# Expert layers' routing: every third token tile's row marks on GpSimd, and roundings to tiles in units of rows

## The reference

```python
gate_logits = jnp.einsum('bsd,de->bse', x, gate_kernel)
top_k_weights, top_k_indices = jax.lax.top_k(gate_logits, TOP_K)
top_k_weights = jax.nn.softmax(top_k_weights.astype(jnp.float32), axis=-1)
h0 = jnp.einsum('bsd,edm->bsem', x, wi_0)
h1 = jnp.einsum('bsd,edm->bsem', x, wi_1)
h = jax.nn.silu(h0) * h1 * combine_w[..., None]
out = jnp.einsum('bsem,emd->bsd', h, wo)
```

## Time and profile before

| | us |
|---|---|
| median of three runs | 1566.65 |
| the three runs | 1563.93, 1566.65, 1568.6 |
| the profiled execution's own time | 1566.98 |
| its span on the core | 1565.2 |

### The profile page before, as it was taken

The page is one execution under the profiler, slowest core; times in us unless marked ns, Lnnn a source line. Parts: engine busy times, 40 slices in busy tenths (PEclk is TensorE's granted clock), DMA queues, the critical chain, the costliest instruction groups (busy, mean ns, idle before and its releaser), DMA issues. The chain is left out here.

```text
span 1565.2 us, 29271 instructions
## 1 busy us (share of the span) xinstructions
PE 1348.1 (86%) x7991; PEld 842.9 (54%) x7992; DVE 1026.3 (66%) x2409; ACT 803.1 (51%) x2370; POOL 627.0 (40%) x660
## 2 busy tenths in 40 slices
PE   5889996798689787999979999988996999969993
PEld 3555553466444353666555666654873666645662
DVE  5898986577569847223656888875335888863224
ACT  4677674687410055331107888843442888823330
POOL 3112420999477232771012111113536664215661
PEclk9999998999799789998998999998996999988997
DMA  6130001400100060794200000331552111412225
GB/s 191 46 113 23 19 12 58 162 0 1 37 17 0 5 211 18 239 286 155 88 17 28 24 23 23 107 122 35 157 134 75 56 43 34 175 55 66 83 83 168
DMA packets 96447, 124.80 MB, mean 80 GB/s; under 512 B 11117, under 2 KB 76464, under 8 KB 96112
## 3 DMA queue, kind: packets, MB, share of 16 engines
q1 hardware_dynamic: 85760, 95.80, 19.2%
q0 software_dynamic: 10608, 28.07, 6.3%
HBM read 91.31 MB, written 33.43 MB: 80 GB/s over the span
## 5 line engine op out<-in xcount | busy, mean ns | idle before, releaser
L717 ACT ACTIVATE l0a_prob<-l0a_ps_s,l0a_neg_max 128x128 f32<-128x128 f32 x512 | 137.9, 398 | 70.6 <-DVE l0a_neg_max L559 63.1
L717 ACT ACTIVATE l2a_prob<-l2a_ps_s,l2a_neg_max 128x128 f32<-128x128 f32 x512 | 138.7, 402 | 26.2 <-DVE l2a_neg_max L559 21.5
L219 POOL TENSOR_TENSOR ln_rstd<-ln_var_eps,minus_half 128x4 f32<-128x4 f32 (+1 forms) x14 | 23.1, 1660 | 246.7 <-POOLq L183 216.3
L1160 ACT ACTIVATE l3a_prob<-l3a_ps_s,l3a_neg_max 128x256 f32<-128x256 f32 x256 | 104.5, 482 | 34.0 <-DVE l3a_neg_max L1074 32.5
L559 DVE TENSOR_REDUCE l2a_neg_max<-l2a_ps_s 128x4 f32<-128x512 f32 x128 | 85.7, 684 | 19.8 <-PE l2a_ps_s L815 18.9
L502 POOL TENSOR_TENSOR l2a_k_head<-l2a_kT,head_of_row 128x512 f32<-128x512 f32 x32 | 33.1, 1054 | 157.7 <-DMA l2a_kT<-k_rows 157.7
L568 DVE COPY l0a_probT<-l0a_ps_t 128x512 f32<-128x512 f32 x128 | 84.7, 683 | 14.5 <-PE l0a_ps_t L827 14.4
L1074 DVE TENSOR_REDUCE l3a_neg_max<-l3a_ps_s 128x2 f32<-128x512 f32 x128 | 84.1, 681 | 12.6 <-PE l3a_ps_s L1211 11.7
L559 DVE TENSOR_REDUCE l0a_neg_max<-l0a_ps_s 128x4 f32<-128x512 f32 x128 | 85.5, 683 | 8.9 <-PE l0a_ps_s L815 8.3
L502 POOL TENSOR_TENSOR l0a_k_head<-l0a_kT,head_of_row 128x512 f32<-128x512 f32 x32 | 32.9, 1048 | 138.0 <-DMA l0a_kT<-k_rows 138.0
L1833 PE MATMUL l1a_ps_y<-l1a_kv,l1a_tap 128*128 128x512 f32 x192 | 84.0, 600 | 3.7 <-POOL l1a_kv L1805 3.7
(11 more groups left out here) (490 smaller groups left out, 3493.7 us busy)
## 6 DMA issues: line engine op xcount, KB each, us to landing
expert_results<-zeros SPq DMA_DIRECT2D x1, 8320.0 KB, 26.3
l1f_got<-expert_results SPq DMA_DIRECT2D x16, 512.0 KB, 3.9
expert_results<-l2f_y_sb SPq DMA_DIRECT2D x47, 128.0 KB, 1.7
l1f_w_gu<-in_l1f_w_gu SPq DMA_DIRECT2D x16, 352.0 KB, 6.7
l2f_w_gu_all<-in_l2f_w_gu SPq DMA_DIRECT2D x1, 4096.0 KB, 14.0
l3f_w_gu_all<-in_l3f_w_gu SPq DMA_DIRECT2D x1, 4096.0 KB, 13.9
l3f_got<-expert_results SPq DMA_DIRECT2D x16, 256.0 KB, 5.2
l1f_w_d<-in_l1f_w_d SPq DMA_DIRECT2D x16, 176.0 KB
```

The lines of the kernel that those rows point to most:

```text
L717: last = act.activation(prob[4 * c + j][:, r * P:r * P + P], ps_s[j][:, r * P:r * P + P], ACT.Exp, bias=neg_max[:, j, r:r + 1])
L1160: last = act.activation(prob[4 * c + j][:, m * D:m * D + D], ps_s[j][:, m * D:m * D + D], ACT.Exp, bias=neg_max[:, j, m:m + 1])
```

## The change

Two edits, in all three expert layers.

Row marks: token tiles 2, 5, 8, 11 and 14 are marked by GpSimd, the other eleven by VectorE. GpSimd waits for slot_done, which the slot_row instruction now raises, does its five tiles in order with K instructions each after its first shared multiplications and before it waits for row_out, and keeps the same rule of the ring. TensorE waits for row_marked or for row_marked_by_pool by the tile. slot_row is now the negative of the row, and lane counts down to match.

Roundings: MAGIC_ROWS = 128 * MAGIC rounds a number of rows straight to a multiple of 128. tiles, ends and base are then in rows: the counts take two instructions where they took three, the base needs no multiplication, and slot_tile takes one where it took two and keeps MAGIC_ROWS in it. It is compared with tile_at = 128 * tile_no + MAGIC_ROWS, which one added instruction makes ahead of the wait for place_put. In L2F and L3F one instruction and a drain are added behind the row marks, which divide ends by 128 for the owners. The hunk left out names the two new semaphores.

```diff
--- before.py
+++ after.py
@@ -1286,6 +1286,7 @@
 
 
 MAGIC = 1.5 * 2.0 ** 23
+MAGIC_ROWS = MAGIC * P
 
 
 def hadamard_ffn(core, name):
@@ -1937,7 +1938,7 @@
             from_slot = sb("from_slot", [P, B, K], U32)
         slot_tile, slot_row = sb("slot_tile", [P, B, K]), sb("slot_row", [P, B, K])
         lane, row_of = sb("lane", [P, P], BF16), sb("row_of", [P, 1])
-        tile_no = sb("tile_no", [P, NT])
+        tile_no, tile_at = sb("tile_no", [P, NT]), sb("tile_at", [P, NT])
         in_row = [sb(f"in_row{u}", [P, K, P], BF16) for u in range(RING)]
         marks = sb("marks", [P, B * K, NT], BF16)
         got = [got_all[:, r * K * D:(r + 1) * K * D].rearrange("p (k d) -> p k d", k=K) for r in range(NG)]
@@ -1996,12 +1997,12 @@
...
@@ -2156,7 +2157,7 @@
 
             pool.affine_select(out=before[:, :], in_=before[:, :], compare_op=ALU.is_gt, fill=0.0, base=0,
                                pattern=[[1, P]], channel_multiplier=-1).then_inc(const_done, 1)
-            for out, pattern, rowwise in ((tile_no, [[1, NT]], 0), (lane, [[1, P]], 0), (row_of, [[0, 1]], 1)):
+            for out, pattern, rowwise in ((tile_no, [[1, NT]], 0), (lane, [[-1, P]], 0), (row_of, [[0, 1]], 1)):
                 pool.iota(out[:, :], pattern, base=0, channel_multiplier=rowwise,
                           allow_small_or_imprecise_dtypes=True).then_inc(const_done, 1)
             if not capacity:
@@ -2170,6 +2171,14 @@
 
             for n in range(bounds[2]):
                 shared_mul(n)
+            pool.wait_ge(slot_done, 1)
+            for t in range(2, B, 3):
+                if t >= RING:
+                    pool.wait_ge(tokens_put, t - (RING - 1))
+                for k in range(K):
+                    last = pool.tensor_scalar(in_row[t % RING][:, k, :], lane[:, :], slot_row[:, t, k:k + 1], 1.0,
+                                              ALU.is_equal, ALU.mult)
+                last.then_inc(row_marked_by_pool, 1)
             pool.wait_ge(row_out, B // 4 * 16)
             def put_results(j):
                 if j == 0:
@@ -2283,23 +2292,20 @@
             dve.tensor_tensor(weight[:, :, :], top[:, :, 0:K], best.broadcast_to([P, B, K]), ALU.subtract)\
                .then_inc(max_done, 1)
 
+            dve.tensor_scalar(tile_at[:, :], tile_no[:, :], float(P), MAGIC_ROWS, ALU.mult, ALU.add)
             dve.wait_ge(place_put, 1)
             if capacity:
                 where = ps_p[:, 0:B * E].rearrange("p (t e) -> p t e", t=B)
             else:
 
                 dve.wait_ge(counted, 1)
-                dve.tensor_scalar(tiles[:, :], ps_l[:, 0:E], 127.0, 1.0 / P, ALU.add, ALU.mult)
-                dve.drain()
-                dve.tensor_scalar(tiles[:, :], tiles[:, :], 1.0 / 256 - 0.5, MAGIC, ALU.add, ALU.add)
-                dve.drain()
-                dve.tensor_scalar(tiles[:, :], tiles[:, :], MAGIC, None, ALU.subtract)
+                dve.tensor_scalar(tiles[:, :], ps_l[:, 0:E], (P - 1) / 2, MAGIC_ROWS, ALU.add, ALU.add)
+                dve.drain()
+                dve.tensor_scalar(tiles[:, :], tiles[:, :], MAGIC_ROWS, None, ALU.subtract)
                 dve.drain()
                 dve.tensor_tensor_scan(ends[:, :], ones_e[:, :], tiles[:, :], 0.0, ALU.mult, ALU.add)
                 dve.drain()
                 dve.tensor_tensor(base[:, :], ends[:, :], tiles[:, :], ALU.subtract)
-                dve.drain()
-                dve.tensor_scalar(base[:, :], base[:, :], float(P), None, ALU.mult)
                 dve.drain()
                 dve.tensor_tensor(place[:, :, :], ps_p[:, 0:B * E].rearrange("p (t e) -> p t e", t=B),
                                   base[:, :].unsqueeze(1).broadcast_to([P, B, E]), ALU.add)
@@ -2322,16 +2328,14 @@
                 dve.tensor_tensor(spot[:, :, :], spot[:, :, :], flag[:, :, :], ALU.add)
                 dve.drain()
 
-            dve.tensor_scalar(slot_tile[:, :, :], spot[:, :, :], 0.5 - P / 2, 1.0 / P, ALU.add, ALU.mult)
-            dve.drain()
-            dve.tensor_scalar(slot_tile[:, :, :], slot_tile[:, :, :], MAGIC, MAGIC, ALU.add, ALU.subtract)
+            dve.tensor_scalar(slot_tile[:, :, :], spot[:, :, :], (1 - P) / 2, MAGIC_ROWS, ALU.add, ALU.add)
             dve.drain()
             with nc.allow_low_precision(reason="whole numbers under 256"):
-                dve.tensor_tensor(marks[:, :, :], tile_no[:, :].unsqueeze(1).broadcast_to([P, B * K, NT]),
+                dve.tensor_tensor(marks[:, :, :], tile_at[:, :].unsqueeze(1).broadcast_to([P, B * K, NT]),
                                   slot_tile[:, :, :].rearrange("p t k -> p (t k)").unsqueeze(2)
                                   .broadcast_to([P, B * K, NT]), ALU.is_equal).then_inc(tile_marked, 1)
-                dve.scalar_tensor_tensor(out=slot_row[:, :, :], in0=slot_tile[:, :, :], scalar=-float(P),
-                                         in1=spot[:, :, :], op0=ALU.mult, op1=ALU.add)
+                dve.scalar_tensor_tensor(out=slot_row[:, :, :], in0=slot_tile[:, :, :], scalar=MAGIC_ROWS,
+                                         in1=spot[:, :, :], op0=ALU.subtract, op1=ALU.subtract).then_inc(slot_done, 1)
                 dve.drain()
                 dve.tensor_scalar(in_tile[:, 0, :, :], marks[:, :, :], row_of[:, :], None, ALU.mult)\
                    .then_inc(row_scaled, 1)
@@ -2345,10 +2349,13 @@
                 last.then_inc(row_marked, 1)
 
             for t in range(B):
-                mark_rows(t)
+                if t % 3 < 2:
+                    mark_rows(t)
             if not push:
                 dve.tensor_copy(from_slot[:, :, :], spot[:, :, :]).then_inc(from_done, 1)
             if not capacity:
+                dve.tensor_scalar(ends[:, :], ends[:, :], 1.0 / P, None, ALU.mult)
+                dve.drain()
                 dve.tensor_tensor(past[:, :, :], tile_no[:, :].unsqueeze(2).broadcast_to([P, NT, E]),
                                   ends[:, :].unsqueeze(1).broadcast_to([P, NT, E]), ALU.is_ge)
                 dve.drain()
@@ -2698,7 +2705,10 @@
                 pe.wait_ge(pair_marked, 1)
             for t in range(B):
                 pe.wait_ge(time_marked, t + 1)
-                pe.wait_ge(row_marked, t + 1)
+                if t % 3 < 2:
+                    pe.wait_ge(row_marked, t - t // 3 + 1)
+                else:
+                    pe.wait_ge(row_marked_by_pool, t // 3 + 1)
                 for k in range(K):
                     last = pe.matmul(ps_p[:, 0:NS * NT].rearrange("p (s j) -> p s j", s=NS), in_row[t % RING][:, k, :],
                                      in_tile[:, :, t * K + k, :],
```

More of the change, by code:

```diff
@@ L1998, in moe_ffn @@
         (w_in, sw_in, const_done, row_done, xT_put, xT_done,
-         l_put, l_done, max_done, e_done, chosen_done, place_put, counted, owner_done, tile_marked, row_scaled, pair_marked, time_marked, row_marked, tokens_put, tokens_done, from_done, to_done, gate_e,
+         l_put, l_done, max_done, e_done, chosen_done, place_put, counted, owner_done, tile_marked, row_scaled, pair_marked, time_marked, row_marked, row_marked_by_pool, slot_done, tokens_put, tokens_done, from_done, to_done, gate_e,
          sg_put, s_silu, s_early_mul, s_mul, sd_put, sd_done, in_turned, in_copied, gu_put, e_silu, e_mul, h_turned,
@@ L2003, in moe_ffn @@
              "xT_put", "xT_done", "l_put", "l_done", "max_done", "e_done", "chosen_done", "place_put",
[L2004 removed]
+             "counted", "owner_done", "tile_marked", "row_scaled", "pair_marked", "time_marked", "row_marked", "row_marked_by_pool", "slot_done", "tokens_put", "tokens_done", "from_done", "to_done", "gate_e", "sg_put", "s_silu",
              "s_early_mul", "s_mul",
```

1 line of the change is left out of this document (removed).

## The result

The changed kernel takes **1571.74 us** (median of 9 runs, 1568.89 to 1575.69) against 1566.45 for the kernel before (9 runs, 1563.93 to 1568.6): the ratio is 1.0036 with a 95% interval of 1.0025 to 1.0046, so 5.3 us slower. The forecast was 1564.5, and its range ended at 1570.5. The profiled execution took 1574.02 us, with a span of 1572.2; both kernels' profiled executions had a mean granted clock of 0.935.

A forecast was written before the change was run, and what follows sets the result against it. TensorE, busy 86%, bounds the kernel, so VectorE savings count only where TensorE waits, as in the routings. L3F 1.2, L2F 0.9 and L1F 0 make 2.1 us, giving 1564.5 us; range 1560.0 to 1570.5.

The forecast's parts named there:

- the price of a GpSimd mark: Row marks, all three layers: 0.37 us per 128-column mark on GpSimd, read from its tensor_scalar rows with a pointer scalar.
- the rival: GpSimd late: each GpSimd mark takes 0.6 us more or less surely bounded there, 3.1 us slower, 1569.8; chance 0.11.
- the prediction's own formulas: Marking time from TensorE's start S plus four remaining GpSimd tiles: L3F S + 3.6 instead of S + 4.4, L2F 4.2 us.
- L1F: L1F's marking: gain of 0 to 0.4 us by GpSimd's pace, all taken by port losses, so 0 in the sum.
- GpSimd late: Rival: GpSimd marks cost 0.6 us, TensorE waits for its tiles, 3.1 us slower, 1569.8; chance 0.11.
- Ports in turn: Rival: every GpSimd mark stops VectorE for its full 0.37 us; 5.2 us slower, 1571.9; chance 0.14.
- The 0.15 us per mark: Port loss taken for VectorE per GpSimd mark, from a possible 0.07 to 0.37: 0.4 us in each small layer.
- The roundings: Fewer VectorE instructions ahead of marks: 0.74 us in L3F, 0.3 in L2F; 0.25 comes back behind L3F's marks.
- an earlier rise of the clock: Rival in L2F: shorter marking lets TensorE's clock rise one block sooner, 1.8 us more, 1562.7; chance 0.13.

The follow-up runs named there:

- e3: Kernel before, plus ten forms of tensor_scalar on idle GpSimd ahead of L3F, each twice, into unread buffers; the mark's own form took 0.90 and 0.78 us.
- e8: Changed kernel with GpSimd's comparison replaced by two multiplications with a zero, so every third tile's tokens are left out of the experts; 1566.22 us, ratio 1.0002.
- e5: Kernel before, VectorE making all marks, with GpSimd also making its ten of L2F and L3F into an unread buffer; 1565.55 us, ratio 0.9991.
- e1: Changed kernel with all row marks back on VectorE, merged roundings kept; 1567.43 us, ratio 1.0029.
- e7: Changed kernel with all marks on VectorE and 8 mark buffers (6 in L1F) instead of 4, merged roundings kept; 1564.31 us, ratio 0.9997.
- e12: Changed kernel with all of L1F's marks back on VectorE, L2F and L3F still shared; 1570.06 us, ratio 1.003.
- e10: Changed kernel, unaltered, run a second time; 1571.41 us, ratio 1.0037 against the kernel before.
- e2: Kernel before with only every third tile marked by GpSimd, old roundings kept; 1578.44 us, ratio 1.0086.
- e9: Kernel before with only the in_row ring lengthened from 4 buffers to 6 in L1F and 8 in L2F and L3F; 1561.72 us, ratio 0.9971.

## Why the prediction was wrong, point by point

**The step that failed** is the price of a GpSimd mark: "I take 0.37: 0.74 us per tile of two marks, 1.48 per tile of four", bounded at 260 and 432 ns. It measured 0.709 to 0.744 us, outside its own bounds and above the 0.6 of the rival. e3 shows what went wrong: the rows it was read from the earlier trace rows are pairs of multiplications, and the price was taken to hang on the columns. It hangs on the pair of operations first. The two-input row of 432 ns, taken as the upper bound, is another operation again and bounded nothing.

With the measured price the prediction's own formulas give the marking that came. L3F: GpSimd ends at S + 0.5 + 4 x 1.42 + 0.1 = S + 6.3, where VectorE ended at S + 4.4 before: 1.9 longer, measured 2.1. L2F: 0.85 + 4 x 1.49 + 0.35 = 7.2 us against 5.19, measured 1076.51 to 1083.63, 7.1. For a GpSimd that is late the way of reckoning who waits for whom was right; a wrong input turned the sign, since with five tiles of sixteen GpSimd was the slower engine at 0.37 already and there was no slack for a dearer one. At the price that had been taken the same formulas promise too much. For the share, less the ports, they have 0.6 us in L2F, 0.7 in L3F and nothing in L1F; e8, at 385 ns, has 0.45, 0.15 and 0.4 of loss. In its L3F TensorE stood idle for only 0.46 us in the marking, and its matmuls, twelve of them 1.63 us at a granted clock of 0.50, fill the rest of the 4.74: that TensorE itself would be the limit there was a term the forecast left out. With the price right the sum would have been 1.0 us, 0.8 of it from the roundings, and not 2.1; that is an estimate from e8's stretches. "GpSimd late", held at 0.11, was the rival that came, larger than priced.

**L1F** was the term furthest off: a gain of 0 to 0.4 was expected, 2.2 us of loss by the rival, 5.1 came (27.0 to 32.1). The timeline takes it apart: from TensorE's first marking matmul to the shared block 7.35 us (618.58 to 625.93) against 4.14 before (613.53 to 617.67), 3.2 longer, with two of the waits in it; the shared block 5.61 against 5.14, 0.5 longer, as it ran at the low clock until 630.1, 4.2 us of its length, where before it was 3.3; behind it to the next shared matmuls 4.26 (631.54 to 635.80) against 2.82, 1.4 longer, with the wait for tile 14. Put into the prediction's formula, 0.71 for 0.6 explains 0.9 us of the difference to the rival for tiles 5 and 8 and 0.4 for tile 14; of the 1.6 us that are left, 0.3 are GpSimd's start of tile 5, 0.9 us behind TensorE's first matmul where 0.6 had been taken, 0.5 the longer shared block, and some 0.8 have no account.

**Ports in turn** is refuted, though its 1571.9 lies within 0.2 us of what was measured; a total that fits is no evidence for its mechanism. It asked for VectorE marks near 0.5 us beside GpSimd's, and they stayed at 247 to 255 ns, with e5's full stream at 242. The 0.15 us per mark, 0.4 us in each small layer, that the forecast took for the ports on VectorE's side were too much as well: e5 has 0.03 us per mark and 0.2 in each layer, below the 0.07 that was its lower bound. More is lost on GpSimd's side, 865 against 709 ns in e5. That single instructions do block each other is seen elsewhere: in L2F after, GpSimd's multiplication took 2.70 us behind VectorE's marks instruction of 1.73, against 1.26 before, and slot_row 1.25 us behind it, against 0.18 in L3F. The Trainium skill, SBUF — State Buffer, section "SBUF: two separate sides", says that of a GpSimd instruction and one of VectorE that has two inputs in SBUF or runs in a two-port mode, whichever starts first holds the shared pair of ports for its whole instruction and the other blocks. Those rows agree: marks and slot_row both have two inputs. If VectorE's row marks, which have one, run in such a mode, which no row tells, the rule would have them stand still behind GpSimd's for whole marks of 0.7 us, and the traces don't show that: there VectorE gives way by 0.03 us and GpSimd by 0.12 to 0.16.

**The roundings** were right in mechanism and size at the place they were costed for: TensorE's marking in L3F begins 0.76 us sooner (0.74 expected), in L2F 0.5 in e1 and 0.7 after (0.3 expected), and the ends' division takes back 0.25 ahead of tokens. The rounding that stood behind GpSimd's multiplication stayed pinned, as said: the second one took 1.28 us, as its twin did before. In the profiles of e7 and e12 that multiplication was over before this rounding began; there it took 0.17 us, and the marking of L2F began 1.4 us sooner than before. That the gain would reach the total isn't shown; in e1 the expert loop's first rows were no sooner.

**From 7.5 to 5.3.** From the first rounding of the counts to the end of the marking L2F lost 1.3 us (14.4 to 15.7), to tokens L3F lost 1.1 (12.55 to 13.66), and L1F's routing 5.1: 7.5 us. The total is 5.3, with an interval of 3.9 to 7.2. One place behind L1F where time is given back can be seen in the profiles. In the kernel before, TensorE's granted clock was 0.57, 0.50 and 0.65 in the three windows of 4 us from 716, in the changed one 1.00 in all of them and in the two behind. The first two shared blocks of twelve matmuls there:

```profile
717.25 5.75 PE L2656 MATMUL l1f_ps_l<-l1f_sw_d,l1f_s_hT 128*128 128x256 f32 x12 [0.71 <-DVE l1f_rows L2430]
722.94 4.93 PE L2656 MATMUL l1f_ps_p<-l1f_sw_d,l1f_s_hT 128*128 128x256 f32 x12
```

and after:

```profile
726.93 3.02 PE L2663 MATMUL l1f_ps_l<-l1f_sw_d,l1f_s_hT 128*128 128x256 f32 x12 [0.72 <-DVE l1f_rows L2437]
729.88 3.05 PE L2663 MATMUL l1f_ps_p<-l1f_sw_d,l1f_s_hT 128*128 128x256 f32 x12
```

That is 4.6 us of 10.7 in this pair of executions, and it is not due to the change. From L1F's last gather to the shared part's late multiplications the stage took 36.6 us before and 31.8 after (31.3 in e10, 31.9 in e2), but 32.6 in e3 and 30.7 in e5, whose L1F is the one of before; all other kernels lie between 30.0 and 33.3. So it was the profiled execution of the kernel before that was slow there, and where the total gets its 2 us back stays open. In L1F's marking itself the clock went the other way: it was 0.50 until 630.1 after, where before it was at 1.00 from 621 on. That one does go with the change: the clock rose 11.1 to 11.6 us after the marking's start in after, e10 and e2, 7.5 to 8.3 us after it in before, e1, e3, e5, e8 and e12, and 4.1 to 4.7 us after it in the four kernels with the longer ring. The longer idle pieces of TensorE, 2.24 and 1.80 us, lie in that stretch. The prediction had thought of an earlier rise of the clock, not of a later one. Which part of L1F's 5.1 us is clock and which is waiting was not taken apart.

## What to carry to other kernels

Before work is moved to another engine, look for a row of that very operation on that engine, and not only for its shape; where none is there, the bounds must reach to the dearest operation of that shape that one can imagine, and the split must leave slack for it. Reckon also what the consumer needs by itself: here TensorE's own matmuls left little to gain even at the price that was hoped for (e8). A ring that two engines fill in turn is emptied at the pace of the slower one, so the share of the slow engine is set by (marks per tile) x (its price) against the time in which the consumer takes the tiles between, and nought is a share too. And look at the ring first: two to four more buffers took over 3 us off L1F's routing in four kernels out of four by letting the fast engine run ahead, and 4.5 us off the total in the one set of runs that could tell it (e9), where a second engine cost 5.3.
